# The relation counts of an edge phase: 34 rows of 625 destinations in place of five tiles of 34 columns, and another order of the products

## The reference

```python
seg = edge_type * n + dst
agg = jax.ops.segment_sum(x[src], seg, num_segments=N_REL * n)
cnt = jax.ops.segment_sum(ones, seg, num_segments=N_REL * n)
mean = agg.reshape(N_REL, n, -1) / jnp.maximum(cnt, 1.0).reshape(N_REL, n, 1)
```

## Time and profile before

| | us |
|---|---|
| median of 3 runs | 1664.31 (1662.63 to 1666.99) |
| the profiled execution | 1662.9 |
| its span, from the first to the last instruction | 1660.7 |
| edge phase, to the first VectorE row of the next phase | 190.4 |
| TensorE / VectorE busy over the span | 1335.1 / 935.8 |
| granted clock of TensorE, mean | 0.866 |

### The profile page before, as it was taken

One profiled execution on the slowest core, in us unless ns is written; L12 is line 12 of the kernel. 1 busy time (PEld: TensorE's weight loads), 2 busy tenths in 40 slices (PEclk: granted clock), 3 DMA queues, 4 the chain that ended last, 5 costly groups with the idle time before them and its releaser, 6 DMA issues. The chain is left out here.

```text
span 1660.7 us, 30695 instructions
## 1 busy us (share of the span) xinstructions
PE 1335.1 (80%) x9640; PEld 982.2 (59%) x9641; DVE 935.8 (56%) x1711; ACT 535.8 (32%) x800; POOL 631.6 (38%) x751
## 2 busy tenths in 40 slices
PE   8699385792738489968599999999999938748988
PEld 6477365792634456856366666666666627435666
DVE  8953768685543644034266666566665536666810
ACT  0000320682320433013255554555555423122300
POOL 0077445776665000010355555555555522210000
PEclk9899685696769589988799999999999978958989
DMA  1000200000200421042699998899999865342301
GB/s 56 1 1 2 78 7 10 1 0 1 76 10 1 115 76 38 1 155 82 244 276 292 272 287 250 259 288 276 283 281 289 231 149 171 114 119 88 140 16 31
DMA packets 104209, 210.45 MB, mean 127 GB/s; under 512 B 23571, under 2 KB 48624, under 8 KB 104029
## 3 DMA queue, kind: packets, MB, share of 16 engines
q1 hardware_dynamic: 75484, 145.72, 25.5%
q0 software_dynamic: 28672, 64.04, 16.9%
HBM read 196.71 MB, written 37.22 MB: 141 GB/s over the span
## 5 line engine op out<-in xcount | busy, mean ns | idle before, releaser
L599 PE MATMUL r_pO<-ring,r_rowsT 128*128 x2592 | 433.1, 326 | 0.0
L599 PEld LDWEIGHTS r_pO<-ring,r_rowsT 128*128 128x128 f16 x2592 | 250.7, 98 | 158.4 <-issue 0.2
L1640 DVE SCALAR_TENSOR_TENSOR ring<-q_wstage,ring 128x768 f16<-128x768 f32 x198 | 175.2, 954 | 66.1 <-ACT ring L1599 61.9
L1579 POOL DMA_INDIRECT acc_dram<-r_msg,r_scol x72 | 133.0, 1847 | 167.0 <-PE r_pT L1700 98.0
L1599 ACT ACTIVATE ring<-q_wstage 128x768 f16<-128x768 f32 x198 | 148.8, 829 | 39.8 <-issue 25.0
L442 POOL DMA_INDIRECT inv_col<-qinv_dram,pair_col x112 | 120.0, 1072 | 79.3 <-POOL pair_col L455 74.4
L392 POOL DMA_INDIRECT slot_dram<-table_record,table_rowi x80 | 101.4, 1268 | 107.8 <-issue 107.2
L355 PE MATMUL acc<-oh_d,oh_s 125*125 125x512 f16 (+1 forms) x800 | 140.8, 316 | 0.0
L1628 ACT ACTIVATE r_msg<-r_pO,slot_inv 128x768 f32<-128x768 f32 x72 | 64.6, 897 | 191.6 <-PE r_pO L599 170.3
L1700 PE MATMUL r_pT<-r_S,q_parts 128*128 128x128 f16 x876 | 104.2, 222 | 24.2 <-DVE r_S L1657 12.6
L1647 DVE TENSOR_TENSOR r_rowsT<-r_pT,r_rowsT 128x512 f16<-128x512 f32 x73 | 50.2, 688 | 123.8 <-ACT r_rowsT L1608 111.7
(11 more groups left out here) (359 smaller groups left out, 2421.0 us busy)
## 6 DMA issues: line engine op xcount, KB each, us to landing
q_wstage<-in_L_gnn_W_rel_dram SPq DMA_DIRECT2D x33, 2304.0 KB
f_stage<-in_L_ffn_w_dram SPq DMA_DIRECT2D x12, 768.0 KB, 5.1
stage<-in_L_gnn_W_dram SPq DMA_DIRECT2D x6, 768.0 KB
q_wstage<-in_L_ffn_w_fast_dram SPq DMA_DIRECT2D x6, 768.0 KB
q_wstage<-in_L_ffn_w_slow_dram SPq DMA_DIRECT2D x6, 768.0 KB
q_wstage<-in_L_ffn_h_fast_dram SPq DMA_DIRECT2D x6, 768.0 KB
f_stage<-in_L_ffn_w_fast_dram SPq DMA_DIRECT2D x6, 768.0 KB, 4.7
f_stage<-in_L_ffn_w_slow_dram SPq DMA_DIRECT2D x6, 768.0 KB, 6.2
```

Source lines behind the costliest of these rows:

```text
L599: ins = eng.matmul(out, x, w[:, h * n:(h + 1) * n], start=first and x is xh and w is wh, stop=last and x is xl, **kw)
L1579: eng.indirect_dma_start(out=K.acc_dram[u % 2], out_offset=bass.IndirectOffsetOnAxis(ap=scol[:, u:u + 1], axis=0), in_=msg[:, u, :], in_of ...
L1640: ins_ = eng.scalar_tensor_tensor(wring[:, slot, 1, k, :], wstage[:, slot, k, :], W_SCALE, wring[:, slot, 0, k, :], ALU.mult, ALU.subtract)
```

## The change

The relation counts are computed the other way round. Before, five products per column with 125 destinations on the partitions of the result and 34 relations as its columns; now the 34 columns of `R` are the stationary side and the 625 destinations the moving side, in two pieces of 312 and 313 columns (`relation_piece`). A column has 12 products in place of 15. The result lies as 34 partitions of 625 numbers, in what is left of bank 6 and in bank 7.

As bank 7 now holds a sum that is open all the time, the prefix sums are added into it beside that sum, on columns that a zero product has opened, and VectorE copies them out at once, into `total_` and `before`. TensorE waits for those copies (`prefix_taken`) before it goes on. So VectorE's wait for the prefix sums moves ahead of the reduction `second`; the copy L257 is gone from its old place.

In the node count, the piece of 113 columns now goes ahead of that of 512 within a tile. The inverses are stored relation by relation, and `slot_columns` works out relation times 625 plus destination.

```diff
-        qinv = sb("qinv", [P, NT, REL], FP32)
+        qinv = sb("qinv", [REL, N], FP32)
...
+            def relation_piece(piece):
+                b, o = ((6, REST), (7, 196))[piece]
+                return acc[0:REL, b, o:o + HALF - 1 + piece], slice(piece * (HALF - 1), (HALF - 1) + piece * HALF)
...
-                eng.dma_start(K.qinv_dram.rearrange("(i p r) a -> p i (r a)", p=P, r=REL), qinv[:, :, :]).then_inc(s["qinv_stored"], 16)
+                eng.dma_start(K.qinv_dram.rearrange("(r n) a -> r (n a)", r=REL), qinv[:, :]).then_inc(s["qinv_stored"], 16)
...
                 hots(HOTS + 13, PREFIX_AT + 4)
+                eng.wait_ge(s["prefix_ready"], 1)
+                eng.tensor_copy(total_[:, :, :].rearrange("p a g -> p (a g)"), acc[:, 7, 128:128 + 2 * REL])
+                eng.tensor_copy(before[:, :, :].rearrange("p a g -> p (a g)"), acc[0:EP, 7, 0:2 * REL]).then_inc(s["prefix_taken"], 1)
+                eng.wait_ge(s["prefix_taken"], 1)
                 link(eng.tensor_reduce(second[:, :], g2(same).rearrange("p g j -> p j g"), AX.X, ALU.add))
-                eng.wait_ge(s["prefix_ready"], 1)
-                total = acc[:, 7, 128:128 + 2 * REL].rearrange("p (a g) -> p a g", a=2)
+                total = total_[:, :, :]
...
-                link(eng.tensor_copy(before[:, :, :].rearrange("p a g -> p (a g)"), acc[0:EP, 7, 0:2 * REL]))
...
-                link(eng.tensor_scalar(qinv[:, :, :], acc[0:P, 6, REST:REST + NT * REL].rearrange("p (i r) -> p i r", r=REL), 1.0, W_SCALE,
-                                       ALU.max, ALU.mult))
-                eng.reciprocal(qinv[:, :, :], qinv[:, :, :]).then_inc(s["qinv_ready"], 1)
+                for piece in range(2):
+                    a, cols = relation_piece(piece)
+                    last = eng.tensor_scalar(qinv[:, cols], a, 1.0, W_SCALE, ALU.max, ALU.mult)
+                link(last)
+                eng.reciprocal(qinv[:, :], qinv[:, :]).then_inc(s["qinv_ready"], 1)
...
+                    for piece in range(2):
+                        a, cols = relation_piece(piece)
+                        eng.matmul(a, onehot, oh_d[:, u, cols], start=False, stop=False, **kw)
                     for t in range(NT):
                         tile = slice(t * P, (t + 1) * P)
-                        at = REST + t * REL
-                        eng.matmul(acc[0:P, 6, at:at + REL], oh_d[:, u, tile], onehot, start=False, stop=False, **kw)
-                        for piece in range(2):
+                        for piece in (1, 0):
                             a, cols = count_piece(t, piece)
                             last = eng.matmul(a, oh_s[:, u, tile], oh_d[:, u, cols], start=False, stop=False, **kw)
...
                 zeros(range(7), P, True, False)
+                zeros((7,), 128, True, False)
...
-                eng.matmul(acc[0:EP, 7, 0:2 * REL], tri[:, :], each, start=True, stop=True)
-                eng.matmul(acc[:, 7, 128:128 + 2 * REL], ones[:, :], each, start=True, stop=True).then_inc(s["prefix_ready"], 1)
+                eng.matmul(acc[0:EP, 7, 0:2 * REL], tri[:, :], each, start=False, stop=False, **kw)
+                eng.matmul(acc[:, 7, 128:128 + 2 * REL], ones[:, :], each, start=False, stop=False, **kw).then_inc(s["prefix_ready"], 1)
+                eng.wait_ge(s["prefix_taken"], 1)
...
-                zeros((6,), P, False, True).then_inc(s["products_done"], 1)
+                zeros((6,), P, False, True)
+                zeros((7,), 128, False, True).then_inc(s["products_done"], 1)
...
-    link(eng.tensor_scalar(tmp[:, :], K.dst_col[:, 0:T1, 0], 0.0, float(REL), ALU.max, ALU.mult))
-    link(eng.tensor_tensor(tmp[:, :], tmp[:, :], relf[:, :], ALU.add))
+    link(eng.tensor_scalar(tmp[:, :], K.dst_col[:, 0:T1, 0], 0.0, None, ALU.max))
+    link(eng.scalar_tensor_tensor(tmp[:, :], relf[:, :], float(N), tmp[:, :], ALU.mult, ALU.add))
```

More of the change, by code:

```diff
@@ L124, in edge_phase @@
         before = sb("before", [EP, 2, REL], FP32)
+        total_ = sb("total", [128, 2, REL], FP32)
         code, second, place, beside = (sb(n, [EP, EJ], FP32) for n in ("code", "second", "place", "beside"))
@@ L139, in edge_phase @@
         s = {n: K.sem("e_" + n) for n in (
-            "edges_loaded", "x_loaded", "consts_ready", "rowcnt_ready", "prefix_ready", "ranks_ready",
+            "edges_loaded", "x_loaded", "consts_ready", "rowcnt_ready", "prefix_ready", "prefix_taken", "ranks_ready",
             "products_done", "counts_stored", "rest_stored", "hots_ready", "hots_free", "transposed",
```

## The result

The changed kernel takes 1686.08 us in the median of 4 runs (1679.52 to 1689.43), the kernel before 1665.65 in 4 runs on the same chip (1662.63 to 1668.30): ratio 1.0118 [1.0082, 1.0155]. It is slower, by more than the forecast (1668.7) and beyond its range (1663 to 1673). The profiled execution of after took 1689.43 us, the highest of its four, and is compared with the 1662.9 of before, which is near the lowest; so the two profiles lie 26.5 us apart where the medians lie 20.4 apart.

What follows compares the result with a forecast made beforehand. The edge phase was taken as bound in turn by VectorE's small steps, TensorE's products and VectorE's tail. +2.4 - 1.6 + 0.2 + 0.5 + 2.8 = +4.4 us gave 1668.7 on the median, range 1663 to 1673.

Steps and rivals of the forecast that it cites:

- TensorE's column: Edge phase products at full clock: a column takes 1.650 us, 0.034 less than before; -1.6 us over 46 columns.
- The pair of slots: Short (113) and long (512) product of a source tile: 0.056 and 0.221, tile 0.277 us, five a column.
- rival 1: Pair of slots stays at 0.285: column 1.690, sum +6.3, 1670.6 us; chance 0.22.
- rival 2: Loads hide wholly, slots 0.050 and 0.215: column 1.59, sum +1.7, 1666.0 us; chance 0.15.
- The half-clock columns: Columns right after TensorE's restart, at half clock: stay as they were, 3.20 us before and after.
- The prefix wait: VectorE's wait and copies, now ahead of the reduction, delay column 28 and the restart at column 32; +2.4 us.
- The eighth bank: One more 512-column zero product at the start and one at the end of the products; +0.2 us.
- the scaling: VectorE's tail: scaling in two pieces over 34 partitions of 625 takes 0.86 instead of 0.36; +0.5 us.
- the reciprocal: VectorE's tail: 625 elements a partition instead of 170, 4.04 us instead of 1.22; +2.8 us.
- the distance from the barrier to the end: Everything behind the edge phase: stays the same; a change of more than 1.5 us would make the prediction wrong.
- Rival 3: Streamed columns decide, 3750 instead of 3295: column 1.874, sum +14.7, 1679 us; chance 0.06.
- Rival 4: Number of products decides, 12 instead of 15: column 1.35, sum -9.5, 1654.8 us; chance 0.07 with a gain from elsewhere.

Runs made afterwards that it cites:

- e1: Changed kernel with the relation products reading 34 columns of a second one-hot laid side by side, built by VectorE in 3.2 us; 1689.38 us, one run.
- e2: As e1, but the relation products load 66 columns of the side-by-side one-hot, result rows beyond 34 unused; 1671.83 us, one run.
- e8: Kernel before with VectorE's table steps moved ahead of its wait for the products and degrees summed tile by tile; 1669.75 us, ratio to before 0.9989.
- e6: Kernel before with only the moved prefix wait and its copies ahead of the reduction; 1677.65 us, ratio to before 1.0034.
- e5: Changed kernel with the reduction put back ahead of VectorE's wait for the prefix sums; 1685.01 us, ratio to before 1.0054.
- e9: As e7, with VectorE's table steps also moved ahead of the wait for the products; 1662.99 us, ratio to before 0.9923.
- e7: Changed kernel with 66 side-by-side relation columns, copied by ScalarE, and the reduction ahead of the wait; 1670.96 us, ratio to before 0.9978.
- e10: As e9, with ScalarE's copy of the relation weights in two parts, the first for 8 columns; 1659.67 us, ratio to before 0.9964.

## Why the prediction was wrong

**The step that failed** is in "TensorE's column": two products of 0.13 "are 0.265, and they cover both loads of the relation one-hot". They do not cover them: the relation's load starts with its own product, and so does the next load of 125 columns. The two products and what they do to their neighbours cost 0.58 a column (0.093 + 0.212 + 0.229 + 0.046), 0.31 more than forecast. Over 46 columns that is the whole distance from -1.6 to +12.7, 14.3 us. e1 and e2 show that it is the change of shape, 34 columns among 125 (0.25), and the stride (0.07). I had asked whether a load is long enough to be covered, and not whether the engine starts it under a running product at all.

The trace of before had a place that shows it, which I did not read. Next to the 313-column products of rows 8 stand four whose stationary side is 8 rows high; products, then loads:

```profile
1559.67 0.70 PE L1352 MATMUL f_mps<-f_xT,ring 128*128 128x313 f16 x4
1560.34 0.71 PE L1345 MATMUL f_mps<-f_wT,f_sel 8*128 8x313 f16 x4
1560.98 0.31 PE L1352 MATMUL f_mps<-f_xT,ring 128*128 128x313 f16 x1
```

```profile
1560.33 0.38 PEld L1345 LDWEIGHTS f_mps<-f_wT,f_sel 8*128 x4 [0.29 <-issue]
1560.97 1.06 PEld L1352 LDWEIGHTS f_mps<-f_xT,ring 128*128 x9 [0.26 <-issue]
```

Four products take 0.64 (1560.34 to 1560.98) where four times 0.13 is 0.53, and at both changes of shape the load unit is idle until the next product's start. The 0.1 is the price of one change; a column has two, so the row could have priced the relation term at 2 x 0.1 a column, +9 us, of the 14 that it came to. The shape differs in its rows there and in its columns here, and both changes cost 0.09.

**The pair of slots** (5 x 0.277): right. Its intervals are 0.054 and 0.222, together 0.276, which also puts rival 1 (0.285) and rival 2 (0.265) out. The rows of loads that it was worked out from are coarse: start to start of the products, the intervals before are 0.044, 0.241 and 0.053, so an exposed load had been under 0.05, and the long slot over 0.23. The sum was not hurt by it. The Trainium skill, "TensorE: Matmul & The Clock Gate", section "LDWEIGHTS (loading the stationary operand)", would make the short slot 0.104; 0.054 at full clock does not agree. The Trainium skill, same page, section "The mechanism", has a load pulled ahead of a running product where it goes to other rows of the array or to a background weight buffer, and its list of what overlaps names other rows alone. e2, whose loads all cover the same 125 rows and start up to 0.22 ahead of their products, does not agree with the list; whether the buffer is the reason no run here shows.

**The half-clock columns** (no change forecast): the same step costs there too. The pair of relation products is 0.68 long (90.06 to 90.74), and column 32 takes 3.54 instead of 3.23. But most of the 1.7 is another thing: the granted clock over column 33 was 0.93 in before and 0.56 in after, so that column took 1.82 and 3.23. When the clock comes back differs between profiles of one kernel: e8, the same as before up to there and with the same restart at 85.69, took 6.25 for the two columns where before took 5.05. Against e8 the change costs 0.5, and the other 1.2 can't be laid to it.

**The prefix wait** (+2.4): right by itself, 2.5 in e6; it came to 4.4 because the columns ahead of it are slower too, a consequence of the same step. That its mechanism was the uncovered reduction e5 shows: with the reduction first, 3.9 of the 4.4 us at column 32 are back, and VectorE's idle time falls to 0.44.

**The eighth bank, the scaling, the reciprocal**: 0.2, 0.5 and 2.8 forecast; 0.2, 0.5 and 2.8 measured (0.86 less 0.36, 4.06 less 1.22). The inverse count's new addresses cost nothing that can be seen behind the barrier. The prediction had called itself wrong if the distance from the barrier to the end changed by more than 1.5 us; it changed by 4.2, but with profiles from 1470 to 1479 that sign was set too tight to say anything.

**Rival 3** (1679, column 1.874) came nearest in number, with the wrong cause: it is not the streamed columns, which e2 streams at 1.647. The formula that it takes from the Trainium skill, same page, section "Back-to-back issue gap", is given there for an isolated product, and the section says that in a stream with loads it counts too little for short ones: so does the 1.41 for a column of 1.684. **Rival 4** failed: fewer products are not faster by their number.

## What to carry to other kernels

Before products are regrouped, look at the shape of each stationary side, not only at the columns streamed: among loads of one shape a product of 312 columns costs its streaming (0.135 us measured in e2, 0.130 by the clock), and one odd shape costs 0.09 us on the way in and again on the way out; padding the operand (66 for 34 columns among 125) takes that away without a price on TensorE. A wait that is hidden by a long step stays hidden only as long as it stands behind that step. And work that needs nothing from the longest engine's result belongs ahead of the wait for it, not behind.

## What the runs showed of the hardware that I had not expected

**Loads and shapes.** At full clock, with the load of the next product of another shape: 0.315 for 0.222 behind a 512-column product, 0.229 for 0.136 behind a 313-column one; and the short product after it 0.100 for 0.049. A strided stationary side of 34 columns (160 bytes apart) costs 0.068 more than one side by side, behind a 312-column product.

**GpSimd's scatters beside VectorE.** The scatters into the table take 1.2 us each, one every 1.5. In e9 one took 4.96, 3.8 more. (The gap of 2.4 ahead of it is another thing: it stands once in the row of scatters of every kernel, in before at 150.13, with no long step on VectorE.) First GpSimd, then VectorE:

```profile
156.76 4.96 POOL L410 DMA_INDIRECT slot_dram<-table_record,table_rowi  x1 [2.39 <-issue]
162.03 1.19 POOL L410 DMA_INDIRECT slot_dram<-table_record,table_rowi  x1 [0.31 <-issue]
```

```profile
156.54 4.12 DVE L299 TENSOR_TENSOR c<-iota_t,tin 128x3808 f32<-128x3808 f32 x1
160.69 4.12 DVE L300 TENSOR_REDUCE table_relf<-c 128x112 f32<-128x3808 f32 x1
```

The scatter starts 0.2 after VectorE's step with two inputs and ends 1.1 after it, and the next one, beside the reduction with one input, is as short as ever. The Trainium skill, "SBUF — State Buffer", section "SBUF: two separate sides", says that VectorE with two inputs from SBUF and a GpSimd operation that reads SBUF exclude each other for a whole instruction; this pair of rows agrees. A step with one input was not always harmless: in e7 a scatter that started at 172.91, 1.0 into the reciprocal of 4.06 with the two-input step right behind it, took 8.10, while in before one beside the shorter reciprocal took 1.19; no run tells why. In e9 and e10, where GpSimd most likely ends last, the 3.8 us are not free: VectorE's idle time before the barrier is 1.3 us longer there than in before.
